# Waits and signals of two attentions by single head instead of by pair

## What is computed

```
sim  = einsum('bhid,bjd->bhij', q, k) + bias        # 16 heads, 512 x 512, causal
attn = softmax(sim)                                 # with one null key in front
out  = einsum('bhij,bjd->bhid', attn, v) -> @ Wo -> layernorm
```

```
full_mask = (block_scores(q_mean, k_mean) > THRESH) | eye
scores    = where(full_mask, einsum('bhid,bhjd->bhij', q, k) * SCALE, -inf)
attn      = softmax(scores)
smask     = attn's maximum over each 64 x 64 block > THRESH | eye
out       = einsum('bhij,bhjd->bhid', where(smask, attn, 0), v) @ wo
```

## Time and profile before

| | |
|---|---|
| median of three executions | 2753.78 us (2753.34 to 2756.57) |
| profiled execution, its own time | 2752.22 us |
| its span in the profile | 2750.4 us |
| PE busy | 2598.3 us, 94% |
| DVE, ACT, POOL busy | 52%, 38%, 33% |
| conditioned attention of layer 0 (units) | about 58 to 475 us |
| gated attention | about 515 to 925 us |
| conditioned attention of layer 1 (units) | about 1760 to 2180 us |

### The profile page before, as it was taken

One profiled execution on the slowest core, in us unless ns is written; L12 is line 12 of the kernel. 1 busy time (PEld: TensorE's weight loads), 2 busy tenths in 40 slices (PEclk: granted clock), 3 DMA queues, 4 the chain that ended last, 5 costly groups with the idle time before them and its releaser, 6 DMA issues. The chain is left out here.

```text
span 2750.4 us, 36762 instructions
## 1 busy us (share of the span) xinstructions
PE 2598.3 (94%) x13249; PEld 1524.6 (55%) x13249; DVE 1432.5 (52%) x3215; ACT 1057.8 (38%) x2459; POOL 913.1 (33%) x953
## 2 busy tenths in 40 slices
PE   7999998889998899999999999999999899899998
PEld 4465655533333348748758658556555557544456
DVE  7466564466667344234243233555645577655545
ACT  4767675344544211111121111265656545311222
POOL 3656564177778122102103102465555210000000
PEclk9999999889999899999999999999999999999998
DMA  4000000000000330000000010233323100400000
GB/s 154 1 1 1 1 1 20 11 10 11 12 13 9 102 129 0 1 0 1 0 0 1 0 41 1 88 116 92 119 77 112 37 1 1 127 0 2 2 10 26
DMA packets 82619, 91.91 MB, mean 33 GB/s; under 512 B 14982, under 2 KB 66064, under 8 KB 82313
## 3 DMA queue, kind: packets, MB, share of 16 engines
q1 hardware_dynamic: 82120, 89.04, 10.4%
q0 software_dynamic: 320, 0.52, 0.1%
HBM read 83.19 MB, written 2.14 MB: 31 GB/s over the span
## 5 line engine op out<-in xcount | busy, mean ns | idle before, releaser
L1013 POOL TENSOR_TENSOR cb_sc<-cb_toep,cb_mk 128x128 f32<-128x128 f32 (+3 forms) x256 | 215.8, 871 | 194.5 <-ACT cb_pr L1051 183.4
L1013 POOL TENSOR_TENSOR cb_bias<-cb_bias,cb_mk 128x128 f32<-128x128 f32 (+3 forms) x256 | 215.2, 871 | 153.6 <-DMA cb_bias<-in_fside_16xSxS 153.3
L399 PE MATMUL PS<-ident,cb_pr 128*128 128x128 f32 x1280 | 195.6, 284 | 24.0 <-ACT cb_pr L1051 21.7
L1652 DVE TENSOR_REDUCE gb_bmax<-PS 128x16 f32<-128x1024 f32 x128 | 156.4, 1224 | 110.8 <-PE PS L1431 110.5
L399 PEld LDWEIGHTS PS<-ident,cb_pr 128*128 128x128 f32 x1280 | 135.9, 141 | 115.8 <-issue 104.8
L700 DVE CUSTOM_DVE_ANT_0 cb_sc<-PS,cb_sc,cb_sneg 128x128 f32<-128x128 f32 (+3 forms) x256 | 130.0, 548 | 125.5 <-PE PS L388 124.2
L3305 POOL TENSOR_TENSOR eb_S<-ff_h 128x1024 f32<-128x1024 f32 x16 | 38.0, 2376 | 465.7 <-PE PS L2225 465.6
L1431 PE MATMUL PS<-gb_ks,gb_qs 32*128 32x512 f32 x512 | 150.2, 675 | 33.6 <-DVE gb_bmax L1652 28.5
L1810 ACT ACTIVATE gb_pt<-PS 128x1024 f32<-128x1024 f32 x128 | 130.4, 1023 | 133.8 <-PE PS L1437 127.3
L700 DVE CUSTOM_DVE_ANT_0 cb_bias<-PS,cb_bias,cb_sneg 128x128 f32<-128x128 f32 (+3 forms) x256 | 129.4, 547 | 89.7 <-PE PS L388 88.8
L1058 ACT ACTIVATE cb_pt<-PS 128x128 f32<-128x128 f32 (+3 forms) x448 | 162.4, 409 | 34.8 <-PE PS L399 34.3
(11 more groups left out here) (557 smaller groups left out, 5052.1 us busy)
## 6 DMA issues: line engine op xcount, KB each, us to landing
cb_bias<-in_fside_16xSxS SPq DMA_DIRECT2D x64, 256.0 KB, 2.9
cb_bias<-in_fside_16xSxS SPq DMA_DIRECT2D x64, 192.0 KB, 2.5
ff_h<-in_L_ffn_h_w SPq DMA_DIRECT2D x2, 4096.0 KB, 23.0
cb_bias<-in_fside_16xSxS SPq DMA_DIRECT2D x64, 128.0 KB, 2.2
cb_toep<-rel_table SPq DMA_DIRECT2D x8, 512.0 KB, 7.5
cb_bias<-in_fside_16xSxS SPq DMA_DIRECT2D x64, 64.0 KB, 2.3
ff_w<-in_L_ffn_w_w SPq DMA_DIRECT2D x3, 1024.0 KB, 8.0
gb_ks<-ga_room SPq DMA_DIRECT2D x64, 32.0 KB, 2.0
```

Of the source, the lines that this page charges most:

```text
L399: ins = pe.transpose(PS[:, bank, j * P:j * P + P], pr[:, v % 2, e, j * P:j * P + P], ident)
L1013: ins = pool.tensor_tensor(biases(v, e), turned(h, n) if L0 else biases(v, e), mk[:, b % 2, packed(t):packed(t) + n], ALU.add)
L1652: dve.tensor_reduce(bmax[:, n % 2, t, g:g + 2, 0:NB], PS[:, bank:bank + 2, :].rearrange("p g (n k) -> p g n k", k=64), AX.X, ALU.max)\
```

## The change

Every signal and wait of this path is now per head.

- Conditioned: DVE raises `ca_D` and ACT raises `ca_X` after each head. `scores` waits for `ca_D` of the same head of v-2, `exponential` for `ca_D` of its own head and for the same head's turn of v-2, `turn` for `ca_X` of its own head. No computing instruction is added. PE's `ca_S` stays one per unit.
- Gated: the reduction over two banks becomes two over one bank each, and so does the exponential. `gt_S`, `gt_T`, `gt_M`, `gt_E` are raised per head; in a burst each of the four products waits for the bank that it writes. POOL's additions wait per head.
- All other waits on these semaphores have their numbers doubled (null differences, row sums, POOL's and SP's reuse of bias buffers, denominators, values, maxima).

```
             def scores(v):                                  # conditioned, PE
...
-                if v >= 2:
-                    pe.wait_ge(sm["ca_D"], v - 1)
                 for e in range(2):
+                    if v >= 2:
+                        pe.wait_ge(sm["ca_D"], 2 * (v - 2) + e + 1)
...
             def turn(v):                                    # conditioned, PE
                     bank = ring.put(pe, ("p", v, e))
-                    if e == 0:
-                        pe.wait_ge(sm["ca_X"], v + 1)
+                    pe.wait_ge(sm["ca_X"], 2 * v + e + 1)
...
             def exponential(v):                             # conditioned, ACT
-                act.wait_ge(sm["ca_D"], v + 1)
-                if v >= 2:
-                    ring.wait_filled(act, ("p", v - 2, 1))
                 for e in range(2):
                     k = place(2 * m + e)
-                    ins = act.activation(pr[:, v % 2, e, 0:n], biases(v, e), ACT.Exp,
-                                         bias=nm[:, b % 2, t, k:k + 1], scale=-1.0, accum_out=rs[:, b % 2, t, k:k + 1])
-                ins.then_inc(sm["ca_X"], 1)
+                    act.wait_ge(sm["ca_D"], 2 * v + e + 1)
+                    if v >= 2:
+                        ring.wait_filled(act, ("p", v - 2, e))
+                    act.activation(pr[:, v % 2, e, 0:n], biases(v, e), ACT.Exp, bias=nm[:, b % 2, t, k:k + 1], scale=-1.0,
+                                   accum_out=rs[:, b % 2, t, k:k + 1]).then_inc(sm["ca_X"], 1)
...
             def scores(x, y):                               # gated, PE
-                    if x > 1:
-                        pe.wait_ge(sm["gt_M"], x - 1 if x < UNITS else x)
...
-                    if y:
-                        pe.wait_ge(sm["gt_E"], y)
...
                 for e in range(2):
                     if x < LAST:
+                        if x > 1:
+                            pe.wait_ge(sm["gt_M"], 2 * (x - 2 if x < UNITS else x - 1) + e + 1)
...
-                        if e:
-                            ins.then_inc(sm["gt_S"], 1)
+                        ins.then_inc(sm["gt_S"], 1)
                     if 0 <= y < LAST:
+                        if y:
+                            pe.wait_ge(sm["gt_E"], 2 * (y - 1) + e + 1)
...
-                        if e:
-                            ins.then_inc(sm["gt_T"], 1)
+                        ins.then_inc(sm["gt_T"], 1)
...
             def block_maxima(n, i):                         # gated, DVE
-                dve.wait_ge(sm["gt_S"], UNITS * n + i + 1)
                 bank = first_bank(UNITS * n + i)
-                dve.tensor_reduce(bmax[:, n % 2, t, g:g + 2, 0:NB],
-                                  PS[:, bank:bank + 2, :].rearrange("p g (n k) -> p g n k", k=64), AX.X, ALU.max)\
-                   .then_inc(sm["gt_M"], 1)
+                for e in range(2):
+                    dve.wait_ge(sm["gt_S"], 2 * (UNITS * n + i) + e + 1)
+                    dve.tensor_reduce(bmax[:, n % 2, t, g + e, 0:NB],
+                                      PS[:, bank + e, :].rearrange("p (n k) -> p n k", k=64), AX.X, ALU.max)\
+                       .then_inc(sm["gt_M"], 1)
...
             def probabilities(n, i):                        # gated, ACT
-                act.activation(pt[:, n % 2, g:g + 2, t, :], PS[:, bank:bank + 2, :], ACT.Exp)\
-                   .then_inc(sm["gt_E"], 1)
+                for e in range(2):
+                    act.wait_ge(sm["gt_T"], 2 * (UNITS * n + i) + e + 1)
+                    act.activation(pt[:, n % 2, g + e, t, :], PS[:, bank + e, :], ACT.Exp).then_inc(sm["gt_E"], 1)
```

More of the change, by code:

```diff
@@ L699, in biased @@
                     k = place(2 * m + e)
-                    ins = dve.tensor_tensor_reduce(out=biases(v, e), in0=PS[:, 2 * (v % 2) + e, 0:n], in1=biases(v, e),
-                                                   scale=-1.0, scalar=sneg[:, b % 2, t, k:k + 1], op0=ALU.add,
-                                                   op1=ALU.min, accum_out=nm[:, b % 2, t, k:k + 1])
-                ins.then_inc(sm["ca_D"], 1)
+                    dve.tensor_tensor_reduce(out=biases(v, e), in0=PS[:, 2 * (v % 2) + e, 0:n], in1=biases(v, e),
+                                             scale=-1.0, scalar=sneg[:, b % 2, t, k:k + 1], op0=ALU.add, op1=ALU.min,
+                                             accum_out=nm[:, b % 2, t, k:k + 1]).then_inc(sm["ca_D"], 1)
             def move(v):
@@ L1420, in scores @@
                         pe.wait_ge(sm["gt_qin"], 64 * (n + 1))
-                    if x > 1:
-                        pe.wait_ge(sm["gt_M"], x - 1 if x < UNITS else x)
-                if 0 <= y < LAST:
-                    if y % UNITS == 0:
-                        ring.wait_emptied(pe, ("nm", y // UNITS))
-                    if y:
-                        pe.wait_ge(sm["gt_E"], y)
+                if 0 <= y < LAST and y % UNITS == 0:
+                    ring.wait_emptied(pe, ("nm", y // UNITS))
                 for e in range(2):
                     if x < LAST:
+                        if x > 1:
+                            pe.wait_ge(sm["gt_M"], 2 * (x - 2 if x < UNITS else x - 1) + e + 1)
                         n, t, g = x // UNITS, x % UNITS // 2, 2 * (x % 2) + e
```

23 lines of the change are left out of this document (11 added, 12 removed).

## The result

The changed kernel runs in 2726.11 us (median, 2719.48 to 2728.76, four runs) against 2754.80 us (2753.34 to 2756.57) for the kernel before beside it: ratio **0.9889**, 95% interval 0.9872 to 0.9905. A second series, with the experiments, gave 0.9911 (0.9887 to 0.9935; what stands in brackets behind a ratio is always its 95% interval). The forecast was 2736 us with a range of 2722 to 2751. Sign and range held; the gain is 24 to 31 us where 18 were forecast. The profiled execution took 2728.76 us, with a span of 2726.8.

The account below looks back on a forecast made before the run. PE was taken to bound all three attention stages, idle 80.5 us in them. Conditioned 14 plus gated 4 gives 18 us off 2752.22, 2734; the median lies 1.6 higher, so 2736 us, range 2722 to 2751.

Parts of the forecast that it names:

- Part 1: Conditioned attentions: turn, exponential and scores by head take 14 us off 21.7 us of PE's waits; bounds 7 and 21.7.
- 0.64 of each stall: Conditioned turns waiting for exponentials: mean saving of two stall shapes, nearly 90% and 38%, applied to all 32 stalls.
- rival 2: Stalls move to PE's next wait: conditioned 7, gated 1, 2746 us (chance 0.19), or 2749 and above (0.13).
- Part 2: Gated attention: bursts, maxima and exponentials by head win 4 us; bounds 3 us lost to 9 us won.
- A stall that stands alone: Gated burst waiting for maxima, no stall in the next unit: the split loses 0.06 us.
- Two stalls in a row: Gated bursts stalling in two successive units: the early first pair wins about 0.24 us.
- The clock: PE's clock, at its higher level nearly throughout the three stages (0.99, 0.95, 1.00), was priced at nothing.
- The increments: Gated bursts raise four semaphores, not two: taken to overlap and cost nothing; otherwise 0.05 us per chain, 2.7 us.
- Rival 1: Gated bursts: increments go one after another, the gated term falls by 2.7 us, 2739 us; chance 0.12.
- Rival 3: All idle the change can reach goes: conditioned 21.7, gated 9 us, time 2723 us; chance 0.12.
- Rival 4: Gated second reduction sets the chain, 53 chains 11 us longer; decides if conditioned gives under 11; 2760 us with 5; chance 0.07.
- The fear that a late pair holds up the array: Gated bursts: a pair started late might hold the array its full 1.14 us, costing each split burst up to 0.5 us.

Follow-up runs that it names:

- e2: Only the gated attention's hunks of the change, against the kernel before: ratio 0.9947 (0.9927 to 0.9967).
- e3: Kernel before with four semaphore increments per burst in place of two, readers waiting for twice the number, against the kernel before: ratio 0.9995 (0.9983 to 1.0007).
- e4: e2, but PE waits for both banks ahead of all four products of a burst; against the kernel before: ratio 1.0012 (0.9998 to 1.0026).
- e5: Conditioned part of the change alone, but ACT's exponentials wait for both heads; against the kernel before: ratio 0.9979 (0.9963 to 0.9994).
- e6: Conditioned part of the change alone, but PE's turns wait for both exponentials; against the kernel before: ratio 0.9981 (0.9967 to 0.9994).
- e7: e2 with the exponential left whole, so only the reduction is split by bank; against the kernel before: ratio 0.9968 (0.9956 to 0.9980).

## Why the prediction was right, and where its sizes were off

**What bounds the kernel**: held. PE stays the bound, and the gain is below what it was idle.

**Part 1, 14 us**: about 12 by the stages, 10.6 at equal clock. The step "0.64 of each stall" was wrong in both directions. (Its 38% for a late ACT is 35% by its own 0.3 of 0.86 us, which would make the term 13.3 us.) Of the stalls at the turns 89% went (21.7 to 2.3), not 64%. The shape of the earlier trace rows is the common one: in 22 of the 32 stalls of before the first head's exponential was there, signal included, before PE fell idle, and in the other ten PE had waited 3.2 of their 10.0 us for it. Then the wait at the values grew by 7.9 us, rival 2's mechanism, to which the sum gave nothing (only the lower bound had it). The two errors nearly cancel. "PE's waits fall to about 8 us" failed, "each stage shortens by about 7" came out as 5.5 and 6.2.

**Part 2, 4 us**: 9 to 10, and 15 with the clock. The pieces of its working were right. The second bank's chain: 0.60 from start to start and 0.69 each, measured 0.608 and 0.684. A stall that stands alone: 2.47 us from burst end to burst end became 2.49, 0.02 lost where 0.06 were forecast. Two stalls in a row: the median over 15 of them went from 4.94 to 4.68 us, 0.26 won where 0.24 were forecast. Wrong was what it was counted on. The records before show 54 chains that closed within 0.1 us of the reduction's end: 20 alone, 15 doubles and one run of four. That is one double in each group of eight units, the low end of my one to two; added up they give 5.2 us for the doubles, 0.9 for the run of four and nothing for those alone. But the other 73 intervals, which I had left at zero, lost 7.0 us too (243.3 to 236.4, some of it by the clock). The one I looked at closely went from 2.67 to 2.23 us: its burst came 0.25 us behind the reduction's end, and it followed on a stall. An early pair helps there as well, and a rule that knows only "alone" and "in a row" misses it. Without the clock, taking only intervals that ran at the higher level in both kernels: the stalls won 3.6 us (48 of 54), as good as the forecast's 4, and the others 2.8 (66 of 73). So what was missing in the working is the second term.

**The clock** was priced at nothing because it stood near its higher level, at 0.95 in the gated stage. That was the other missing step: the profiled execution of before spent 36.9 us of the gated stage at the lower level, and the executions with the new code 16 us less than those with the old, on average. The two groups do not overlap (16.4 to 35.9 us with the new waits, 36.8 to 49.6 with the old ones), and over whole executions e2 spent 12.6 us less at the lower level than before, the changed kernel 17.5. The table by execution also shows the other direction: the conditioned part alone spent 11.4 us more. No run tells why. So a gain of 4 to 10 us of the 24 to 31 is the clock's, found and not explained.

**The increments**: I took them to overlap ("if they overlap it is nothing, which I take"). They do not, e3 shows 26.5 ns each. The sum was not hurt, because in the changed kernel the readers are still busy with the first bank when the last ones come.

**Rivals.** Rival 1: mechanism real, price not paid. Rival 2: real in the conditioned part, 7.9 us. Rival 3's 2723 came nearest in time (2726.11), by luck: not all idle went, and part of the gain is the clock's. Without the clock's part, that is with the 20 to 21 us of the waits alone, the time would be about 2733, nearest to the forecast's 2736. Rival 4's pieces exist (1.31 against 1.283 us per chain, and e4 at 1.0012 shows what they cost without the early start), and its point of decision was not reached. The fear that a late pair holds up the array for its full length fell: pairs 0.18 apart overlap.

## What to carry to other kernels

Signals by bank paid most here when every wait in the consumer's in-order stretch was by bank: splitting one stream of an interleaved burst won 4 us or lost 8, and both together won 10 (at equal clock). Do not read the gain from the wait table: a wait can move to the next consumer, or turn into "busy" time in which one product holds an array that four could share; compare the stage's length. Then take out the clock: set each execution's time beside its time at the lower level, or two edits that differ by 5 us look the same, as e5 and e6 did. And a stall that stands alone loses a little from a split, stalls in a row win, and so do bursts that come just behind a stall.

## What the runs showed of the hardware

- Increments of products that end together go one after another, 26 ns each (0.057 to 0.110 us with two more, median of 128). The kernel's ratio does not show it (0.9995); at equal clock it is 1.1 us.
- An exponential started on the first bank's signal goes with a start of the reduction on both banks that is 0.07 us later (0.110 to 0.18 us, with and without PE's waits among the products), and reductions started on the first bank's signal with a start of the exponential on both banks that is 0.047 us later (0.145 to 0.192 us, e3 and e7).
- Two reductions of 512 columns in a row take 0.608 + 0.684 = 1.29 us against 1.224 for one of 1024; two exponentials 1.09 against 1.02.
- The same gated code took 394.1 to 399.8 us in four executions, by how long PE's clock was at its lower level (36.8 to 49.6 us): about 0.4 us of length for each us. Over 213 whole executions it is 0.41.
